# A gated cross-attention block: w and the gated z transposed through DRAM and 32x32 blocks in samples 3 to 6, and the passes in a new order

## The reference

```python
# attention: inp_q = layernorm(x), inp_k = inp_v = ctx
t = einsum('oc,bcd->bod', Wt, inp_v); p = einsum('oc,bcd->bod', Wp, inp_q); g = einsum('oc,bcd->bod', Wg, inp_k)
att = sum(pg * gg, axis=-1, keepdims=True)          # one number for each group of 32 channels
y = einsum('goi,bgid->bgod', Wzg, att * tg)         # block diagonal mix
yn = (yg - mu) * rsqrt(var + EPS);  attn = yn * gn_w + gn_b + residual
x = x + tanh(g_xattn) * attn(layernorm(x), ctx, ctx)
# expert layer on layernorm(x)
z = einsum('bsd,nd->bsn', x, A_w)                   # 512 wide
z_gated = z * gate                                  # softmax over the top 16 of 64 scores
out = einsum('bsn,on->bso', z_gated, B_w) * SCALING
x = x + tanh(g_ffn) * out
```

## Time and profile before

| what | value |
|---|---|
| time, median of 3 runs | 338.32 us (337.33 to 364.02) |
| time of the profiled execution | 338.32 us |
| its span, first to last instruction | 336.5 us |
| PE busy | 329.8 us, 98% of the span |
| DVE busy | 234.5 us, 70% |
| ACT busy | 160.3 us, 48% |
| POOL busy | 151.6 us, 45% |
| moved by DMA | 47.49 MB, mean 141 GB/s |
| granted TensorE clock | 1.000 |

### The profile page before, as it was taken

How to read it: one execution, slowest core, us unless ns; L and a number is a source line. 1 busy time by engine, 2 the same in 40 slices (tenths; PEclk the granted TensorE clock), 3 DMA queues, 4 the chain that set the end, 5 groups by cost and what they waited for, 6 DMA issues and landing times.

```text
span 336.5 us, 5636 instructions
## 1 busy us (share of the span) xinstructions
PE 329.8 (98%) x2060; PEld 298.6 (89%) x2060; DVE 234.5 (70%) x616; ACT 160.3 (48%) x286; POOL 151.6 (45%) x146
## 2 busy tenths in 40 slices
PE   7989999999999999999999999999999999999995
PEld 6588998899988998889988999889998899889984
DVE  0867995875779657895588837896577965774362
ACT  2678934884355623483255802737225652146010
POOL 0154897399165544547153480654626453000000
PEclk9999999999999999999999999999999999999999
DMA  7999703951905137051641508133190110002002
GB/s 249 411 387 400 297 0 92 354 181 34 337 6 175 76 96 280 1 204 50 183 191 48 204 3 298 77 105 145 54 323 2 62 65 0 0 2 112 15 31 94
DMA packets 15179, 47.49 MB, mean 141 GB/s; under 512 B 1824, under 2 KB 1952, under 8 KB 15152
## 3 DMA queue, kind: packets, MB, share of 16 engines
q1 hardware_dynamic: 14800, 46.93, 39.0%
q10 hardware_dynamic: 352, 0.20, 0.2%
HBM read 38.74 MB, written 8.39 MB: 140 GB/s over the span
## 4 chain that ended last, share of the span: by engine, by line
PE 92%; DMA 3%; DVE 1%; SPq 1%; ACT 1%; issue 1%; ACTq 0%; DVEq 0%
PE z_ps L1003 27%; PE w_ps L1031 18%; PE w_ps L929 11%; PE w_ps L886 10%; PE w_ps L1038 9%; PE t_ps L986 4%; PE w_ps L1003 4%; DMA c_sb<-in_ctx 3%; PE z_ps L955 3%; PE t_ps L1017 2%; PE z_ps L871 2%; DVE c_lo L783 1%; PE z_ps L942 1%; PE t_ps L897 0%; ACT c_hi L409 0%
## 5 line engine op out<-in xcount | busy, mean ns | idle before, releaser
L1031 PE MATMUL w_ps<-B_hi,zT_hi 128*128 128x512 f32 x128 | 52.5, 410 | 0.0
L294 POOL TENSOR_TENSOR xT_lo<-xT_in,xT_hi 128x512 fp32r<-128x512 f32 x24 | 30.5, 1293 | 48.7 <-ACT xT_hi L391 48.7
L1031 PE MATMUL w_ps<-B_lo,zT_hi 128*128 128x512 f32 x128 | 50.1, 391 | 0.0
L1003 PE MATMUL z_ps<-A_hi,hT_hi 128*128 128x288 f32 x224 | 48.4, 298 | 0.2 <-ACT hT_hi L456 0.2
L1003 PE MATMUL z_ps<-A_lo,hT_hi 128*128 128x288 f32 x224 | 48.0, 296 | 0.0
L1003 PEld LDWEIGHTS z_ps<-A_hi,hT_hi 128*128 128x128 f32 x224 | 36.3, 189 | 1.1 <-ACT hT_hi L456 0.5
L1003 PEld LDWEIGHTS z_ps<-A_lo,hT_hi 128*128 128x128 f32 x224 | 35.9, 188 | 0.0
L1003 PE MATMUL z_ps<-A_hi,hT_lo 128*128 128x288 f32 x224 | 34.5, 296 | 0.0
L1038 PE MATMUL w_ps<-B_hi,zT_lo 128*128 128x512 f32 x128 | 34.5, 392 | 0.0
L1003 PEld LDWEIGHTS z_ps<-A_hi,hT_lo 128*128 128x128 f32 x224 | 31.4, 189 | 0.0
L294 POOL TENSOR_TENSOR cT_lo<-cT_in,cT_hi 128x512 fp32r<-128x512 f32 x24 | 30.5, 1293 | 0.0
(11 more groups left out here) (147 smaller groups left out, 761.3 us busy)
## 6 DMA issues: line engine op xcount, KB each, us to landing
c_sb<-in_ctx SPq DMA_DIRECT2D x16, 512.0 KB, 5.0
x_sb<-in_x SPq DMA_DIRECT2D x16, 512.0 KB, 6.0
xT_in<-in_xT SPq DMA_DIRECT2D x14, 512.0 KB, 6.7
cT_in<-in_cT SPq DMA_DIRECT2D x14, 512.0 KB, 7.5
out_block<-uw SPq DMA_DIRECT2D x14, 512.0 KB, 2.9
A_in<-in_aT SPq DMA_DIRECT2D x8, 256.0 KB, 12.4
B_in<-in_bT SPq DMA_DIRECT2D x8, 256.0 KB, 10.1
xT_first<-in_xT SPq DMA_DIRECT2D x2, 512.0 KB, 9.6
```

What stands on the lines that cost most here:

```text
L294: last = pool.tensor_tensor(lo[:, chunks, :], came[:, chunks, :], hi[:, chunks, :].bitcast(f32), ALU.subtract)
L1003: last = pe.matmul(banks[i][:, 0:ZH], (hT_lo if low else hT_hi)[:, t, k * P:k * P + P], w[:, k, i * ZH:(i + 1) * ZH], start=(k == 0 and no ...
L1031: pe.matmul(w_ps[k][:, :], zT_hi[:, t, row], w[:, j, cols], start=(j == 0 and w is B_hi), stop=False)
```

## The change

In samples 3 to 6, w is not transposed on PE. SP writes each tile of `uw` to a DRAM scratch in four column blocks (512 pieces of 1 KB) and, when that has landed, reads it back as 128 rows of 4 KB into `c_sb`; this moves whole 32-row groups to the right partitions. What is left is a transpose within 32x32 blocks, which DVE does (`hT_turn`, two instructions a tile, from `c_sb` to `t_ps`). The gated z goes the same way in samples 2 to 6 (`zT_turn`, one instruction a tile, through one buffer that was `products`), but for tile 1 of sample 6. The other transposes stay on PE. Since this gives chunk j of the columns the features 8p + j (for z: 4p + j) at partition p, the weights `A`, `B` and `wq` are laid out so on the host, and the transposes that stay on PE, and `first_w`, read their rows with a step of 8 elements (for z: 4). `att_reduce` writes its products in place in PSUM.

The passes have a new order. In the loop, now over b = 2 to 6, PE does both z_products of b one after the other (tile 1 in `w_ps[0:2]`), then u_product(m) with tile 1 first and n_product(m) in its midst, then the gram of sample m + 1 with group_means(m) and group_att_var(m) in its midst, and then the four out_products. b = 1 has an order of its own, which holds two grams, and b = 6 another, which holds none. DVE, ACT, POOL and SP follow.

```diff
         def gram_bank(n, t):
-            return z_ps[t] if n < 2 else w_ps[t]
+            return w_ps[T + t] if n == 2 else z_ps[t]
...
+        def turned_h(n):
+
+            return 3 <= n < NB - 1
+
+        def turned_z(t, n):
+            return 2 <= n < NB - 1 and not (t == 1 and n == NB - 2)
...
+        def parts(a):
+
+            return a.rearrange("p (c j) -> p j c", c=P)
...
+            def write_z(t, n):
+                sp.wait_ge(zg_done, per_tile(n, t))
+                sp.dma_start(z_scratch[t], zg_sb[:, :].rearrange("p (i d) -> p i d", i=4)).then_inc(z_out[t], 16)
+
+            def read_z(t, n):
+                sp.wait_ge(z_out[t], 16 * (n - 1))
+                if t > 0:
+                    sp.wait_ge(zT_done, per_tile(n, t - 1))
+                elif n > 2:
+                    sp.wait_ge(zT_done, per_tile(n - 1, T - 1))
+                sp.dma_start(z_turned, z_rows[t]).then_inc(z_back[t], 16)
+
+            def write_w(t, n):
+                sp.wait_ge(w_done, per_tile(n, t))
+                sp.dma_start(w_scratch[t], uw[n % 2][:, t, :].rearrange("p (i d) -> p i d", i=4)).then_inc(w_out[t], 16)
+
+            def read_w(t, n):
+
+                sp.wait_ge(w_out[t], 16 * (n - 2))
+                sp.dma_start(c_sb[n % 2][:, t, :], w_rows[t]).then_inc(w_back[t], 16)
...
                 y_root(m)
                 if m + 1 < NB:
-                    xT_low(1, m + 1)
+
+                    pool.wait_ge(w_done, per_tile(m, T - 1))
+                    c_low(m + 1)
                 w_root(m)
                 if m + 1 < NB:
-                    cT_low(1, m + 1)
+                    x_shift(m + 1)
...
+            def hT_turn(t, n):
+
+                dve.wait_ge(w_back[t], 16 * (n - 2))
+                rows = c_sb[n % 2][:, t, :].rearrange("p (g c j) -> p g j c", g=4, c=32)
+                for g in range(NH):
...
+                    dve.transpose(t_ps[g][:, :].rearrange("p (j r g) -> p g j r", j=4, g=4),
+                                  rows[:, :, g * 4:g * 4 + 4, :]).then_inc(hT_done, 1)
+                hT_low(t, n)
+
+            def zT_turn(t, n):
+                dve.wait_ge(z_back[t], 16 * (n - 1))
...
+                dve.transpose(t_ps[0][:, :].rearrange("p (j r g) -> p g j r", j=4, g=4),
+                              z_turned.rearrange("p (g c j) -> p g j c", g=4, c=32)).then_inc(zT_done, 1)
...
+                    rows = parts(uw[n % 2][:, t, :])
                     for k in range(4):
-                        d = (4 * g + k) * P
-                        last = pe.transpose(t_ps[g][:, k * P:k * P + P], uw[n % 2][:, t, d:d + P], ident[:, :])
+                        last = pe.transpose(t_ps[g][:, k * P:k * P + P], rows[:, 4 * g + k, :], ident[:, :])
...
-                    last = pe.transpose(t_ps[0][:, k * P:k * P + P], zg_sb[:, k * P:k * P + P], ident[:, :])
+                    last = pe.transpose(t_ps[0][:, k * P:k * P + P], parts(zg_sb[:, :])[:, k, :], ident[:, :])
```

More of the change, by code:

```diff
@@ L185, in u_tiles @@
         def u_tiles(n):
-            return (1, 0) if n == 1 else range(T)
+            return (1, 0) if n > 0 else range(T)
         def u_uses(n):
@@ L430, in M_high, with u_copy @@
                                    scale=x_rs[:, t:t + 1]).then_inc(M_hi_s, 1)
-            def u_copy(n):
+            def u_copy(n, tiles=range(T)):
                 for k in u_uses(n):
                     t, cols = use(k)
+                    if t not in tiles:
+                        continue
                     if k % NH == 0:
@@ L440, in u_copy, with w_square @@
                                    bias=neg_u[:, t:t + 1]).then_inc(u_copied, 1)
-            def w_square(n):
-                for t in range(T):
+            def w_square(n, tiles=range(T)):
+                for t in tiles:
                     act.wait_ge(w_done, per_tile(n, t))
@@ L826, in _ @@
             hT_low(1, 1)
-            for b in range(1, NB - 1):
+            minus_means(2)
+            gate(0, 1)
+            gram_fix(2)
+            M_low(2)
+            zT_low(0, 1)
+            x_plus_ctx(2)
+            gate(1, 1)
+            u_statistics(2)
+            att_reduce(2)
+            group_deviation(2)
+            slopes(2, lambda: zT_low(1, 1))
+            w_tiles(2)
+            add_out(0, 1)
+            add_out(1, 1)
+            hT_low(0, 2)
+            add_out(2, 1)
@@ L828, in _ @@
+            x_stats(3)
+            gram_fix(3)
+            M_low(3)
+            hT_low(1, 2)
+            add_out(3, 1)
+            minus_means(3)
+            for b in range(2, NB - 1):
                 m = b + 1
-                if m > 2:
-                    x_stats(m)
-                minus_means(m)
+                x_plus_ctx(m)
                 gate(0, b)
-                gram_fix(m)
-                M_low(m)
-                zT_low(0, b)
-                x_plus_ctx(m)
-                gate(1, b)
@@ new lines, in _ @@
+                att_reduce(m)
+                u_statistics(m, (0,))
+                group_deviation(m)
+                slopes(m, lambda: zT_turn(0, b))
+                w_tiles(m)
+                zT_low(0, b)
+                if b < NB - 2:
+                    minus_means(m + 1)
+                    zT_turn(1, b)
+                    zT_low(1, b)
+                    gram_fix(m + 1)
+                    M_low(m + 1)
+                    add_out(0, b)
+                    add_out(1, b)
+                    hT_turn(0, m)
+                    add_out(2, b)
+                    hT_turn(1, m)
+                    add_out(3, b)
+                else:
+                    gate(1, b)
+                    add_out(0, b)
+                    zT_low(1, b)
+                    add_out(1, b)
+                    hT_low(0, m)
+                    add_out(2, b)
+                    add_out(3, b)
+                    hT_low(1, m)
@@ L1025, in out_product @@
                     pe.wait_ge(u_copied, u_use(n + 1, k))
+                if k == USES - 1 and 1 <= n < NB - 2:
+                    pe.wait_ge(cb_s, n + 3)
                 for j in range(KN):
@@ L1118, in rows, with blocks @@
         return a.reshape(2, 128, -1).transpose(1, 0, 2)
+    def blocks(a):
+        return a.reshape(128, a.shape[0] // 128, -1).transpose(1, 0, 2)
     def columns(a):
```

292 lines of the change are left out of this document (209 added, 83 removed).

## The result

The changed kernel takes **354.77 us** (median of 4 runs, 352.63 to 357.63) against 339.19 us of the kernel before on the same chip: ratio **1.0456**, 95% interval 1.041 to 1.0502, slower. I had forecast 330.1 us. Its profiled execution, the longest of the four, took 357.63 us with a span of 355.6.

The account below looks back on a forecast made before the run. PE was taken to bound the kernel, with DVE's new loop of 38.0 us a little over PE's 37.1. 338.3 - 11.2 (transposes removed) + 2.7 (PE waiting for DVE) + 0.3 (b = 6) = 330.1 us, range 326 to 341.

Parts of the forecast that it names:

- What bounds, and what leaves PE: PE never waits once started, so removing 100 transposes takes 11.24 us off; a full pass loses 2.70 us.
- X = 0.68: Time in us of one 128x512 block transpose on DVE, from rows of 0.64, with a far bound of 1.36.
- Steps on PE at nothing: The 92 transposes left on PE read rows 32 or 16 B apart at no cost; bound 10.0 us.
- Where the wait appears: DVE's loop of 38.0 us makes PE wait 0.9 us a pass, three times, in front of `group_means`: 2.7 us.
- C's part on DVE: DVE's stretch from the next sample's first gate to u's statistics done: gates, x's and u's statistics, product sum; 13.24 us.
- part A: DVE's stretch from u's statistics done to kappa, 7.67 us, including two small matmuls with the way back at 0.28 each.
- Meetings with POOL: DVE steps with two SBUF operands wait for POOL: x plus ctx 2.0 us, beta 0.35, w none.
- b = 2 starts with DVE early: Before the loop first closes, x plus ctx is done before b = 2's first z_product ends, so no wait was counted.
- `first_w` at nothing: Reading `first_w` with a step costs no time, hidden because PE is still in u_product(1).
- The load of x at nothing: Loading x later in the queue costs no time; its statistics are asked for over 3 us after issue.
- Number 3: Rival: steps through memory cost on one engine only, PE 340.1 us or DVE 340.3 us; chance 0.14.
- Number 4: Rival: steps through memory cost on both PE and DVE, 350.3 us, slower than before; chance 0.08.

Follow-up runs that it names:

- unit_steps: Changed kernel with DVE's block transposes reading and writing with unit steps instead of 16-byte steps: 338.09, 343.48, 343.70 and 344.19 us.
- unit_read: Changed kernel with DVE's block transposes reading SBUF with unit steps, still writing PSUM with 16-byte steps: 339.83 us in one run.
- order_alone: Changed kernel's order and layout without the trip through DRAM, PE transposing everything: 342.58 us, ratio 1.0074 to the kernel before.
- warm_clock: Changed kernel with sixteen matmuls into an unread bank ahead of PE's wait for the second gate, samples 3 to 6: 348.5 us, ratio 1.0284.
- experiment 1: Changed kernel with unit steps in DVE's block transposes, on both sides (unit_steps) or only in their reads (unit_read, 339.83 us).
- c_low_early: order_alone with `first_w` in contiguous halves, minus_means(3) early on DVE and c_low(3) ahead of x_root(3) on POOL: 340.06 us, ratio 1.0027.
- entry_and_order: order_alone with `first_w` in contiguous halves, minus_means(3) early on DVE and x_shift(3) ahead of c_low(3) on POOL: 345.88 us, ratio 1.0183.
- pool_behind_x: Changed kernel with POOL's eight subtractions for the next sample waiting until x plus ctx is done on DVE: 352.67 us, ratio 1.0427.

## Why the prediction was wrong

The profiled execution is 27.5 us over the sum. Three passes at 44.1 for 38.0 us are 18.3 us; b = 2 adds 3.6 (1.88 us of waiting, and 1.7 by which the twelve matmuls behind it are slower, 138.35 to 142.79 or 4.44 us for 2.73), the start 3.0 (the first z_product of sample 1 at 71.84 against 68.80), b = 6 0.9. 1.7 us stay unplaced.

- **What bounds, and what leaves PE: right.** 100 transposes fewer; z's part alone gives 0.95 us a pass (0.88 predicted) once nothing waits.
- **X = 0.68, wrong, and the largest failure.** It is 1.17 and 1.12, and with 0.70 in its place (unit_steps) 11 us or more come back. I took the nearest rows by shape; their elements lie side by side, and the transposes' do not. My bound of 1.36 held. I also wrote that these reads are 16 bytes apart: w's are 32, only z's 16. The Trainium skill (SBUF — State Buffer, "Door 1: The DMA port swizzle") has an access that goes to a new 16-byte line each time pay. By that rule the price of DVE's read was to be expected, and unit_read bears it out; writes to PSUM with steps of 16 bytes cost nothing measurable, and on PE only the weight loads grew, as the next item has it.
- **Steps on PE at nothing: right.** A weight load takes 0.190 and 0.206 us for 0.140, but eight transposes of w take 0.88 us of the stream in order_alone (0.87 and 0.95 before), and four of z 0.47 (0.44 before).
- **Where the wait appears: wrong, the second failure.** It stands in `u_product`, 14.2 us in four waits, and not in front of `group_means`. I listed what each engine does, but not what each matmul's bank waits for. `u_product` has a wait for `zg_done` that was in the code; with it, C's part on DVE ahead of tile 0 is the first place that shows DVE late.
- **The price of waiting: missed.** I counted a wait once. warm_clock shows 6.3 us for the clock behind the waits alone. With this and the meetings the miss stays at 8 us or more even where X is 0.70 (experiment 1).
- **The small matmuls of part A: wrong.** I had 0.28 us each from the end of DVE's step to the next; they took 0.60 and 0.68. My figure began with PE's matmul and left out the way from DVE's step to it.
- **Meetings with POOL: half right.** x plus ctx took 4.36 us (2.47 + 2.0 predicted), w none. `x_ve` (1.26 for 0.17 us) was not in my list: it reads SBUF alone with two columns and still ran until POOL's subtraction ended. In the other passes the step behind it, `neg_x`, took 1.31 to 1.34 us for 0.15.
- **b = 2 starts with DVE early: wrong**, by c_low(3) on POOL, 5.0 us that I had not walked; with `first_w` 1.6 to 2.5 us in the time (order_alone against c_low_early).
- **`first_w` at nothing: wrong by about 1 us.** Its three first steps take 3.44 us in order_alone and 2.08 in entry_and_order, and w of sample 1 starts 33.3 and 32.5 us behind them (before: 32.4). The other 1.9 us of the later start in the profiled execution lie ahead of `first_w` (32.17 against 30.29) and differ from run to run.
- **The load of x at nothing: wrong** once x plus ctx is late: it is a link of 4.5 us in the chain of each pass.
- **Round trip hidden: right**, with no wait on it in the changed kernel.
- **Rivals.** Number 3's half on DVE (X = 1.36, 340 us) was the mechanism, but with too low a price, as it held neither the clock nor the second meeting. I had written that from X = 1.2 on DVE takes back all that PE gives; it was near that point, and the waits came on top. (The sum there gives 3 x 3.5 = 10.5 us, not 10.9.) Number 4 had 350.3 us, the nearest to the measured time, but with PE's transposes at double their length, which did not happen; that it comes near is luck.

## What to carry to other kernels

Before work moves from a full engine to one at 70%, walk the second one's loop with every wait and ask how much it can take: here two of six steps a pass fitted, and with these two alone, and the start repaired, the kernel beats the one before by 1.1%. Price a moved step by a row with the same memory steps, not only the same shape, and look up for every matmul which semaphore frees its bank. A wait in front of matmuls can cost its length and then the slow clock behind it, here behind waits of 1.7 to 4.2 us, and not behind one of 1.4. When a repair only moves the wait, two ways of nearly equal length are there; here taking load off the engine helped where reordering it did not.

## What the runs showed of the hardware

- DVE, 128x512 float32: block transpose from SBUF 0.70 us with unit steps, 1.12 with reads of 4 bytes 16 apart, 1.17 with 32 apart; steps of 16 bytes in the write to PSUM change nothing. `first_w` (SBUF, steps of 32 bytes on three operands) 1.24 us (order_alone) against 0.75 (entry_and_order).
- PE: weight loads of 128x128 with steps of 32 or 16 bytes 0.190 and 0.206 us against 0.140, hidden in the stream of transposes.
- A DVE step of two columns took 1.26 us beside a running subtraction on POOL (219.85 to 222.36) and 0.17 without; in pool_behind_x two such steps took 0.97 and 1.32.
- Behind a wait of 4.16 us `u_product`'s twelve matmuls took 5.24 us, behind one of 1.88 us 4.44, and with matmuls filling the wait 2.72. Behind a wait of 1.36 us (order_alone) they took 2.86.
